# Output products of 512 columns in passes over two tiles of tokens, and mean and deviation spread over the partitions by two products a block

## The chip, the cores and the metric

The program runs on one core of a Trainium2 chip. The metric is the device time of one execution in microseconds (us). The median of three executions of the kernel before is 2492.5 us (2488.48 to 2496.61).

## The reference, cut to what matters

The input x has 4 sequences of 1024 tokens with 1024 numbers each. It is normalised without gains (`xn`), and the output is `x + attention(xn) + experts(xn)`.

- Attention: `q = xn @ Wq`, `v = xn @ Wv`; `s[t] = lam * s[t-1] + v[t]` along a sequence, with one `lam` a head; `y = q * s`. Then y is normalised over its 1024 numbers (mean mu, variance var), `y = (y - mu) * rsqrt(var + 1e-5) * ln_g + ln_b`, multiplied by `silu(xn @ Wg)`, and multiplied by `Wo`.
- Experts: a router picks 8 of 64 experts for a token. Each expert takes at most 128 of its tokens, computes `h = silu(xg @ w1.T) * (xg @ v1.T)` (384 numbers), then `h @ w2`, and adds the weighted result to the output rows of its tokens.

All products are to be of fp32 quality.

## The kernel before, in words

Every operand of a product is split in a high part (fp32r, written by ScalarE) and a low part (raw less high, written by VectorE or GpSimd). A product is three matmuls into one PSUM accumulation: high by high, high by low, low by high (`three`, L1542 to L1546). K is 1024, so 8 slices k of 128 rows.

The 4096 tokens are walked in 8 blocks j of 512 (4 tiles of 128). In a block, in the order in which TensorE's program is written:

1. The v and q stage (`vq_proj`, L1613): 16 products of 128 channels by 512 tokens (24 matmuls each) into the two banks of `psA`. VectorE runs the scan on v and multiplies by q into `yb` (channels on partitions, tokens on columns). ScalarE squares, GpSimd sums.
2. The gate stage (`g_proj`, L1620): 8 products for Wg. `token_sums` turns the sums into mean and mean square a token, `token_var` and `token_six` compute m (mean) and d (deviation, sqrt(var + eps)) a token and place them, high and low, in six columns of `tok6`; `token_turn` transposes them into `tok6T`. Since 1/d is a factor of the whole row, it is left to the end: with `z = ((y - m) * g + d * b) * gate`, the output is `z @ Wo / d`. So `shift` (L1701) makes, for each chunk m of 128 channels, one 512 column product of `ln6T` (the gains and offsets in six rows) by `tok6T`, which is `d * b - m * g`; `shift_in` (L1196) computes `yb * g + that` in one VectorE instruction that reads PSUM, `gate_in` (L1203) multiplies by the gate, `z_hi_of` and `z_lo_of` split z (chunk 7's low part is VectorE's, `lo_z7`).
3. The out stage (`out_proj`, L1628): z is the stationary side (128 channels by 128 tokens), Wo the moving one. For each quarter mm of the output columns (256 of 1024) and each pair w of token tiles: 2 tiles x 8 k x 3 matmuls of 256 columns into one bank of `psA`, half a bank a tile. `out_copy` (L804) moves a bank to `ot` with the factor 1/d, and `add_out` (L618) adds 512 tokens x 256 columns to the output in DRAM by an accumulating DMA of GpSimd's queue.

Beside the attention's stages run 64 experts: 10 to a block from block 2 on (4 in v and q, 2 in the gate stage, 4 in the out stage), 3 in the out stage of block 1. The expert steps stand between the attention's products in a fixed order: `hidden_turn` (transposes of h), `output_mm` (18 matmuls of 512 columns), `gather_turn` (8 transposes), `hidden_mm` (48 matmuls of 384 columns). An expert's weights come in 6 pieces of 768 KB through three slots (`ew_raw`, `ew_hi`, `ew_lo`); the attention's weights come in pieces of 512 KB through two slots (`pw_raw`, `pw_hi`, `pw_lo`). SyncE's queue issues these loads, each after a wait for the slot.

Block 0 also has the routing of all 32 token tiles between its products, and between block 0's out stage and block 1's gate stage VectorE sorts the routing keys: `list8` (a MAX8 and a MATCH_REPLACE8 over 2048 columns, 16 rounds), then `merge8` (16 rounds over 256 columns). TensorE transposes the merged list (L1780), VectorE computes the index table, and only then can the first expert's rows be gathered. In block 0 the out stage has no experts in it; its weights lie in further rooms (`pw2`, `pw3`), which overlay the buffers of x and the experts.

The order on each engine is the written one; engines meet at semaphores. The waits that matter here: a product waits for the low part of its weights (`s_pwlo`) and for its bank (`s_vq` or `s_go`), the out stage also for z (`s_zlo`, `s_zlo7`), `output_mm` for `shift_in` of the whole block in the gate stage (both use `psY`), `masks_turn` (L1581) for VectorE's top 8 of the last tiles.

Of the kernel before, what the change touches and what calls it, by code (L numbers as in the profile page):

```python
# [52 lines left out]
def build(nc, x, proj_w, ew, router, lam_in, g_in, b_in, out, batches, seq, experts):  # L53
# [16 lines left out]
    with ctx:  # L70
# [8 lines left out]
        slab_bytes = 207 * 1024  # L79
# [13 lines left out]
        ones = place("ones", [P, P], F32)  # L93
# [24 lines left out]
        pw_lo = place("pw_lo", [P, 2, KC, P], F32R)  # L118
        st = place("st", [P, TB], F32)
        sq = place("sq", [P, TB], F32)  # L120
        y_sum = place("y_sum", [P, TB], F32)
        q_sum = place("q_sum", [P, TB], F32)
        tok6 = place("tok6", [P, NT, P], F32)
        tok6T = place("tok6T", [P, TB], F32R)
        ln6T = place("ln6T", [P, KC, P], F32R)
        xn = place("xn", [P, KC, P], F32)
        at_o = top[0]
        ot = place("ot", [P, 2 * NT, 2 * P], F32)
# [6 lines left out]
        at_gT = top[0]  # L135
        gT_hi = place("gT_hi", [P, KC, P], F32R)
        gT_lo = place("gT_lo", [P, KC, P], F32R)
        at_sh = top[0]
        assert at_sh == at_gT + 2 * KC * P * 4
# [5 lines left out]
        end_e = top[0]  # L145
        assert end_e - at_sh >= 2 * KC * P * 4
# [3 lines left out]
        pw2_hi = place("pw2_hi", [P, 2, KC, P], F32R, at_x)  # L150
        pw2_lo = place("pw2_lo", [P, 2, KC, P], F32R, at_x + 2 * KC * P * 4)
        pw3_hi = nc.alloc_sbuf_tensor_at("pw3_hi", [P, 2, KC, P], F32R, offset=slab_at + at_gT, align_bytes=4)
        pw3_lo = nc.alloc_sbuf_tensor_at("pw3_lo", [P, 2, KC, P], F32R, offset=slab_at + at_sh, align_bytes=4)
        rt_hi = place("rt_hi", [P, 2, KC, P], F32R)
        rt_lo = place("rt_lo", [P, 2, KC, P], F32R)
# [19 lines left out]
        ln2 = place("ln2", [P, 2, KC], F32)  # L175
        ln2_hi = place("ln2_hi", [P, 2, KC], F32R)
        ln6 = place("ln6", [P, KC, P], F32)
# [68 lines left out]
        s_ln = sem("s_ln")  # L246
        s_lnT = sem("s_lnT")
        s_l6 = sem("s_l6")
        s_sh = sem("s_sh")
        s_t = sem("s_t")  # L250
# [60 lines left out]
        def each_out(eng, last, body):  # L311

            if last:
                with eng.Fori(0, KC // 2 - 2) as mm:
                    body(mm, True, True)
                body(KC // 2 - 2, False, True)
                body(KC // 2 - 1, False, False)
            else:
                with eng.Fori(0, KC // 2) as mm:
                    body(mm, True, True)  # L320
# [13 lines left out]
        def out_room(mm):  # L334

            return ((pw2_hi, pw2_lo), (pw_hi, pw_lo), (pw3_hi, pw3_lo), (pw2_hi, pw2_lo))[mm]
# [6 lines left out]
        ROUNDS_OUT = (0, 2, 2, 2)  # L343
        ROUNDS_VQ = (3, 3, 2, 2)
# [12 lines left out]
        def _(sp):  # L357
# [51 lines left out]
            def load_first(e):  # L409

                for c in range(3):
                    load_piece(e, c, PIECES * e - 2 + c)
# [43 lines left out]
            for mm in range(KC // 2):  # L456
                if mm == 1:
                    store_w(NB - 1)
                next_xn(0, mm)
                for w in range(2):  # L460
                    load_proj(0, 3 * KC + 2 * mm + w + 4)
                for i in range(2):
                    copy_x(copied + 2 * mm + i)
# [12 lines left out]
            for mm in range(KC // 2):  # L476
                if mm == 0:
                    sp.wait_ge(s_ix, 5)
                    sp.wait_ge(s_wst, 16 * NTILE)
                    sp.wait_ge(s_spare, 48)  # L480
                    for c in range(3):
                        load_piece(0, c)
                next_xn(1, mm)
                if mm > 0:
                    load_rest(mm)
                for w in range(2):
                    load_proj(1, 3 * KC + 2 * mm + w + 4)
                if mm == 0:
                    load_rest(0)
                    load_first(1)  # L490
                else:
# [1408 lines left out]
```

## Time and profile before

| | |
|---|---|
| median of three executions | 2492.5 us |
| profiled execution | 2492.86 us |
| its span (first to last instruction) | 2491.2 us |
| mean granted TensorE clock | 0.992 of full speed |
| TensorE matmul busy | 2440.3 us (98%) |
| VectorE busy | 1628.7 us (65%) |
| ScalarE busy | 1317.3 us (53%) |
| GpSimd busy | 673.4 us (27%) |
| DMA, mean | 243 GB/s |

In a row by stretch stand: its ends and length; busy time (and instructions) of TensorE's matmuls, its weight loads, VectorE, ScalarE and GpSimd; TensorE's granted clock; the DMA engines' busy share; GB/s. A row by group has the line, engine, operation, tiles and shapes, count, busy us, mean ns, and the idle time before it with what ended it. A row of the timeline has start, duration and instruction.

The profile is of one execution; 1.7 us of its time lie outside its span. Ends of matmuls are modelled and overlap, so the time that a matmul costs is read from one start to the next, not from its duration.

### The profile page before, as it was taken

Reading aid. Unit: us, or ns where it says so; the run is one execution under the profiler, and the core shown is the slowest. Engines: PE = TensorE matmul, PEld = TensorE weight load, DVE = VectorE, ACT = ScalarE, POOL = GpSimd, SP = SyncE. Lnnn points to the kernel's source line nnn. Section 1 sums busy time; section 2 is a strip of 40 time slices with the busy share of each in tenths; the row PEclk is TensorE's granted clock in tenths of the full one; section 3 lists DMA queues with packets and bytes.
Section 4 is the critical chain, followed back from the end, with each engine's and each line's share of the span. In section 5 each row is a group of like instructions: output and inputs, shape, how many; then the busy total and the mean of one; then the engine's idle time right before and its main releaser. Section 6 shows DMA issues by size and latency. Waiting matters only on the chain.

```text
span 2491.2 us, 39295 instructions
## 1 busy us (share of the span) xinstructions
PE 2440.3 (98%) x13649; PEld 2185.7 (88%) x13649; DVE 1628.7 (65%) x1689; ACT 1317.3 (53%) x1499; POOL 673.4 (27%) x523
## 2 busy tenths in 40 slices
PE   7999999999999999999999999999999999999997
PEld 7888977898889988899888998889988889988897
DVE  7776897666566666666666766656666566656654
ACT  5557323555456644556445665545654556544554
POOL 3221122223222232222223222322223222323311
PEclk9999999999999999999999999999999999999998
DMA  7786854797668976679766698666986669867686
GB/s 275 261 310 201 243 194 162 240 326 225 203 223 264 304 228 232 221 239 310 252 227 213 214 327 266 218 216 213 307 289 193 233 225 287 277 227 233 208 275 167
DMA packets 151790, 605.74 MB, mean 243 GB/s; under 512 B 20592, under 2 KB 37040, under 8 KB 151216
## 3 DMA queue, kind: packets, MB, share of 16 engines
q1 hardware_dynamic: 116304, 518.91, 57.7%
q0 software_dynamic: 35424, 86.00, 16.7%
q8 instruction: 39, 0.64, 0.1%
q14 instruction: 23, 0.19, 0.0%
HBM read 520.89 MB, written 100.70 MB: 250 GB/s over the span
## 4 chain that ended last, share of the span: by engine, by line
PE 84%; DVE 9%; ACT 3%; DMA 3%; issue 1%; SPq 0%; POOL 0%; DVEq 0%; ACTq 0%; POOLq 0%
PE psA L1544 17%; PE psA L1545 17%; PE psA L1546 17%; PE psH L1544 6%; PE psH L1546 6%; PE psH L1545 6%; PE psY L1544 4%; PE psY L1545 4%; PE psY L1546 4%; DVE ew_lo L1157 3%; PE psX L1651 2%; ACT ew_hi L753 2%; PE psY L1576 1%; DVE keys L1147 1%; DVE l L1144 1%; DVE pw_lo L1152 1%
## 5 line engine op out<-in xcount | busy, mean ns | idle before, releaser
L1157 DVE TENSOR_TENSOR ew_lo<-ew_raw,ew_hi 128x1536 fp32r<-128x1536 f32 x384 | 694.6, 1817 | 331.1 <-ACT ew_hi L753 320.5
L753 ACT ACTIVATE ew_hi<-ew_raw 128x1536 fp32r<-128x1536 f32 x384 | 568.3, 1484 | 162.5 <-DMA ew_raw<-ew_dram 134.4
L1544 PE MATMUL psA<-xT_hi,pw_hi 128*128 128x512 f32 (+1 forms) x1544 | 610.2, 395 | 4.9 <-DVE pw_lo L1152 2.7
L747 ACT ACTIVATE pw_hi<-pw_raw 128x1024 fp32r<-128x1024 f32 x254 | 266.2, 1059 | 640.4 <-PE psA L1546 637.5
L1545 PE MATMUL psA<-xT_lo,pw_hi 128*128 128x512 f32 (+1 forms) x1544 | 602.2, 390 | 0.0
L1546 PE MATMUL psA<-xT_hi,pw_lo 128*128 128x512 f32 (+1 forms) x1544 | 602.0, 390 | 0.0
L1152 DVE TENSOR_TENSOR pw_lo<-pw_raw,pw_hi 128x1024 fp32r<-128x1024 f32 x256 | 315.3, 1242 | 146.7 <-ACT pw_hi L747 141.3
L1544 PE MATMUL psH<-ew_hi,gT_hi 128*128 128x384 f32 x1024 | 345.5, 337 | 4.6 <-DVE ew_lo L1157 4.6
L1544 PEld LDWEIGHTS psA<-xT_hi,pw_hi 128*128 128x128 f32 x1544 | 291.4, 189 | 63.1 <-issue 6.7
L1546 PEld LDWEIGHTS psA<-xT_hi,pw_lo 128*128 128x128 f32 x1544 | 291.2, 189 | 61.7
L1546 PE MATMUL psH<-ew_hi,gT_lo 128*128 128x384 f32 x1024 | 343.0, 335 | 0.0
L1545 PE MATMUL psH<-ew_lo,gT_hi 128*128 128x384 f32 x1024 | 342.7, 335 | 0.0
L1545 PEld LDWEIGHTS psA<-xT_lo,pw_hi 128*128 128x128 f32 x1544 | 291.6, 189 | 56.1
L1544 PE MATMUL psA<-pw_hi,z_hi 128*128 128x256 f32 x1024 | 296.1, 289 | 3.6 <-POOL z_lo L615 2.2
L1546 PE MATMUL psA<-pw_hi,z_lo 128*128 128x256 f32 x1024 | 291.2, 284 | 0.0
L1545 PE MATMUL psA<-pw_lo,z_hi 128*128 128x256 f32 x1024 | 291.0, 284 | 0.0
L601 POOL TENSOR_TENSOR y_sum<-y_sum,yb 128x512 f32<-128x512 f32 x64 | 117.2, 1831 | 546.4 <-ACT sq L790 546.4
L594 POOL DMA_INDIRECT out_dram<-ys,s_idx x64 | 118.6, 1854 | 327.7 <-ACT w_tab L777 303.4
L1544 PEld LDWEIGHTS psH<-ew_hi,gT_hi 128*128 128x128 f32 x1024 | 192.3, 188 | 14.2 <-DVE ew_lo L1157 12.6
L1544 PEld LDWEIGHTS psA<-pw_hi,z_hi 128*128 128x128 f32 x1024 | 197.6, 193 | 4.4 <-POOL z_lo L615 2.4
L1545 PEld LDWEIGHTS psA<-pw_lo,z_hi 128*128 128x128 f32 x1024 | 197.8, 193 | 0.1
L1546 PEld LDWEIGHTS psA<-pw_hi,z_lo 128*128 128x128 f32 x1024 | 197.6, 193 | 0.0
(161 smaller groups left out, 3318.9 us busy)
## 6 DMA issues: line engine op xcount, KB each, us to landing
ew_raw<-ew_dram SPq DMA_DIRECT2D x384, 768.0 KB, 6.3
pw_raw<-proj_w_dram SPq DMA_DIRECT2D x256, 512.0 KB, 5.3
xn_scratch<-xt SPq DMA_DIRECT2D x33, 512.0 KB, 4.7
xt<-x_dram SPq DMA_DIRECT2D x32, 512.0 KB, 6.0
out_dram<-x_dram SPq DMA_DIRECT2D x32, 512.0 KB, 6.2
out_dram<-ot POOLq DMA_DIRECT2D x32, 512.0 KB, 12.5
xn<-xn_turned SPq DMA_DIRECT2D x29, 512.0 KB, 4.2
xn_turned<-xraw SPq DMA_DIRECT2D x28, 512.0 KB, 5.1
```

What stands on the lines that cost most here:

```text
L594: pool.indirect_dma_start(out, bass.IndirectOffsetOnAxis(ap=s_idx[:, 0:1], axis=0), ys[:, :], None, compute_op=ALU.add).then_inc(s_sc, 16)
L601: pool.tensor_tensor(y_sum[:, :], y_sum[:, :], yb[:, 2 * mm + h, :], ALU.add)
L747: act.activation(dst[:, slot, :, :], pw_raw[:, slot, :, :], ACT.Copy).then_inc(s_pwhi, 1)
L753: act.activation(ew_hi[:, c % 3, :], ew_raw[:, c % 3, :], ACT.Copy).then_inc(s_ewhi, 1)
L1144: dve.max(into[:, c], src).then_inc(steps, 1)
L1147: dve.match_replace(src, into[:, c], src, -1.0).then_inc(steps, 1)
L1152: dve.tensor_tensor(dst[1][:, slot, :, :], pw_raw[:, slot, :, :], dst[0][:, slot, :, :].bitcast(F32), ALU.subtract).then_inc(s_pwlo, 1)
L1157: dve.tensor_tensor(ew_lo[:, c % 3, :], ew_raw[:, c % 3, :], ew_hi[:, c % 3, :].bitcast(F32), ALU.subtract).then_inc(s_ewlo, 1)
L1544: pe.matmul(dst, l_hi, r_hi_, start=first, stop=False)
L1545: pe.matmul(dst, l_hi, r_lo_, start=False, stop=False)
L1546: return pe.matmul(dst, l_lo, r_hi_, start=False, stop=last)
L1651: o = pe.transpose(psX[:, k // 4, (k % 4) * P:(k % 4 + 1) * P], xg[:, k * P:(k + 1) * P], ident[:, :])
```

## The change

- Output products: a pass takes one half of the output columns (h, 512 columns) and two tiles of tokens (u). Each of its 16 pairs of k and tile is three matmuls of 512 columns, a tile to a bank of `psA`. There are 4 passes a block, and a pass goes through four pieces q of weights, two k each; Wo is cut on the host so that a piece is 2 k x 512 columns. `out_copy` comes once a pass, after the third expert piece, and copies both banks; in block 0 odd passes use `psH`. `add_out` adds 256 tokens x 512 columns.
- Weights: `pw2` becomes a room of its own for the first two pieces of each half, filled in the gate stage (half 0) and in pass 1 (half 1); `pw` holds the other two. The out stage loads 6 pieces in place of 8, in passes 1, 2 and 3, and the gate stage two more.
- Mean and deviation: the 8 products with `ln6T` give way to 2 a block (`spread`): a product with a matrix of ones and zeros (`sel`) puts m on all partitions, another d. ScalarE makes `d * b` of a chunk into `bs`, with two places (`std_of`), VectorE subtracts m from a chunk (`center`), and `shift_in` is then `yb * g + bs`. `gain_rows` and 6 of 8 transposes at the start go.
- Order: in an out pass `hidden` (and `silu_h`) comes before the split of the last expert piece; `std_of` stands in ScalarE's gate stage; block 1's first gather is issued earlier, its index table is computed in the gate stage, and TensorE's transpose of the merged list stands before the last gate product. In block 0's out stage ScalarE takes the next tokens (`take_xT`) before `logits_lo`, VectorE `xT_lo_of` before `take_logits` and `top8_of`. The 16 rounds of `list8` are spread 4 + 12 (before: 6 + 10) over block 0's out stage and block 1's v and q stage.

```diff
-            def out_proj(j, mm, w, tiles=(0, 1), weights=(pw_hi, pw_lo), ks=range(KC)):
 ...
-                        o = three(psA[:, w, t * 2 * P:(t + 1) * 2 * P], z_hi[:, k, c], z_lo[:, k, c],
-                                  weights[0][:, :, k, :], weights[1][:, :, k, :], k == 0, k == KC - 1)
+            def out_pass(j, h, u, pieces):
+                for q in pieces:
+                    if q == 0:
+                        copies = max(2 * h + u - 1, 0) if isinstance(j, int) and j == 0 else 2 * h + u
+                        pe.wait_ge(s_go, 16 * j + 8 + 2 * copies + 2)
+                    if u == 0:
+                        pe.wait_ge(s_zlo, (KC - 1) * j + min(2 * q + 2, KC - 1))
+                        if q == 3:
+                            pe.wait_ge(s_zlo7, j + 1)
+                        pe.wait_ge(s_pwlo, NPJ * j + 3 * KC + 4 * h + q + 1)
 ...
+                    for kk in range(2):
+                        k = 2 * q + kk
+                        cols = slice(kk * TB, (kk + 1) * TB)
+                        for t in range(2):
+                            toks = slice((2 * u + t) * P, (2 * u + t + 1) * P)
+                            o = three(bank_out(j, u)[:, t, :], z_hi[:, k, toks], z_lo[:, k, toks],
+                                      hi[:, cols], lo[:, cols], k == 0, k == KC - 1)
+                    if q % 2 == 1:
+                        o.then_inc(s_pj, 1)
 ...
-            def shift(j, m):
-                if m > 1:
-                    pe.wait_ge(s_t, KC * j + m - 1)
 ...
+            def spread(j):
+                pe.wait_ge(s_t6, j + 1)
+                ps = psH if isinstance(j, int) and j == 0 else psY
+                for i in range(2):
+                    o = pe.matmul(ps[:, i, :], sel[:, i, :], tok6T[:, :], start=True, stop=True)
+                o.then_inc(s_sh, 1)
 ...
+            def run_out(j, e, h, u):
+                out_pass(j, h, u, range(2))
                 hidden_turn(e)
-                out_proj(j, mm, 1, (0,))
+                out_pass(j, h, u, (2,))
                 output_mm(e)
                 gather_turn(e + 1)
-                out_proj(j, mm, 1, (1,))
+                out_pass(j, h, u, (3,))
                 hidden_mm(e + 1)
 ...
+            def center(j, m):
+                ps = psH if isinstance(j, int) and j == 0 else psY
+                dve.tensor_tensor(yb[:, m, :], yb[:, m, :], ps[:, 0, :], ALU.subtract).then_inc(s_u, 1)
 ...
+            def std_of(j, m):
+                if isinstance(m, int) and m == 0:
+                    act.wait_ge(s_sh, j + 1)
+                if m >= 2:
+                    act.wait_ge(s_t, KC * j + m - 1)
+                ps = psH if isinstance(j, int) and j == 0 else psY
+                act.activation(bs[:, m % 2, :], ps[:, 1, :], ACT.Copy, scale=ln_b[:, m:m + 1]).then_inc(s_bs, 1)
 ...
+            def out_copy(j, i):
+                act.wait_ge(s_pj, n2(j, i, 1) + 1)
+                wait_alone(act, s_acc, 16 * (4 * j + i + 1))
+                for t in range(2):
+                    s = i % 2 * 2 + t
+                    act.activation(ot[:, s, :], bank_out(j, i)[:, t, :], ACT.Copy,
+                                   scale=col[:, 4, s:s + 1]).then_inc(s_go, 1)
```

## Rows read from the trace of the kernel before

**Rows 1.** The page: TensorE's busy time, and the chain that ended last by engine.
```profile
PE 2440.3 (98%) x13649; PEld 2185.7 (88%) x13649; DVE 1628.7 (65%) x1689; ACT 1317.3 (53%) x1499; POOL 673.4 (27%) x523
...
PE 84%; DVE 9%; ACT 3%; DMA 3%; issue 1%; SPq 0%; POOL 0%; DVEq 0%; ACTq 0%; POOLq 0%
```

**Rows 2.** Groups by line and form: out products (one line of three) and shift products.
```profile
L1544 PE MATMUL psA<-pw_hi,z_hi 128*128 128x256 f32 x1024 | 296.1, 289 | 3.6 <-POOL z_lo L615 2.2 <-DVE z_lo L1238 1.3
...
L1706 PE MATMUL psY<-tok6T,ln6T 128*128 128x512 f32 x56 | 18.2, 400 | 0.0
```

**Rows 3.** Timeline of TensorE, out stage of block 2: start, duration, instruction.
```profile
820.15 0.28 PE L1544 MATMUL psA<-pw_hi,z_hi 128*128 128x256 f32 x1
...
825.89 0.49 PE L1671 MATMUL psX<-ident,hh 128*128 128x128 f32 x3
826.14 0.36 PE L1544 MATMUL psA<-pw_hi,z_hi 128*128 128x256 f32 x1
...
829.10 0.40 PE L1544 MATMUL psY<-ew_hi,hT_hi 128*128 128x512 f32 x1
```

**Rows 4.** Timeline of TensorE, v/q and gate stage of block 2: products of 512 columns.
```profile
561.88 0.49 PE L1544 MATMUL psA<-xT_hi,pw_hi 128*128 128x512 f32 x1
...
567.46 0.39 PE L1544 MATMUL psY<-ew_hi,hT_hi 128*128 128x512 f32 x1
...
719.03 0.39 PE L1544 MATMUL psA<-xT_hi,pw_hi 128*128 128x512 f32 x1
...
724.47 0.62 PE L1706 MATMUL psY<-tok6T,ln6T 128*128 128x512 f32 x2
724.92 0.33 PE L1544 MATMUL psH<-ew_hi,gT_hi 128*128 128x384 f32 x1
```

**Rows 5.** Busy time by stretch: block 2's gate and out stage, block 1's v/q, 255 to 263.
```profile
694.60:769.70 75.10, 75.10 (x376) 65.44 (x375) 49.19 (x52) 39.44 (x49) 21.08 (x17) 1.00 0.66 214
769.70:870.20 100.50, 100.50 (x693) 97.23 (x692) 65.05 (x48) 64.64 (x76) 23.36 (x18) 1.00 0.92 292
...
306.30:397.10 90.80, 88.10 (x386) 71.77 (x385) 83.18 (x70) 21.05 (x24) 23.48 (x17) 1.00 0.62 216
...
255.00:263.00 8.00, 6.70 (x32) 6.47 (x31) 5.31 (x15) 0.38 (x1) 0.00 (x0) 0.50 0.61 210
```

**Rows 6.** Groups in block 2's gate stage: nearest rows for the added instructions.
```profile
L1200 DVE SCALAR_TENSOR_TENSOR yb<-yb,ln_g,psY 128x512 f32<-128x512 f32 x8 | 5.7, 740 | 0.0
...
L794 ACT ACTIVATE gb<-psA 128x512 f32<-128x512 f32 x8 | 4.6, 581 | 0.0
```

**Rows 7.** Groups of VectorE from 300 to 400 us, in block 1's v/q stage.
```profile
L1144 DVE MAX8 l<-keys 128x8 f32<-128x2048 f32 x12 | 27.4, 2287 | 0.0
L1147 DVE MATCH_REPLACE8 keys<-l,keys 128x2048 f32<-128x2048 f32 x11 | 25.0, 2276 | 0.0
...
L1193 DVE TENSOR_TENSOR yb<-psA,st 128x512 f32<-128x512 f32 x8 | 5.5, 691 | 3.0 <-PE psA L1546 2.8
```

**Rows 8.** Timeline, block 0's out stage: top 8's last step, next tokens, masks' transposes.
```profile
263.64 0.29 DVE L1096 TENSOR_SCALAR mk<-rep 128x256 f32<-128x256 f32 x1
...
263.70 1.06 ACT L875 ACTIVATE xT_hi<-xn 128x1024 fp32r<-128x1024 f32 x1 [2.43 <-DMA xn<-xn_turned]
...
271.30 0.60 PE L1584 MATMUL psY<-ident,mk 128*128 128x128 f32 x4
```

**Rows 9.** Timeline, block 1: the last merge, and the first expert's transposes.
```profile
439.03 0.41 DVE L1144 MAX8 lf<-l 64x8 f32<-64x256 f32 x1
...
462.21 0.41 PE L1651 MATMUL psX<-ident,xg 128*128 128x128 f32 x2 [3.07 <-DMA xg<-xn_scratch,g_idx]
```

**Rows 10.** Timeline of TensorE, the last expert.
```profile
2472.09 0.90 PE L1671 MATMUL psX<-ident,hh 128*128 128x128 f32 x3 [3.96 <-DVE hh L1162]
2474.16 0.79 PE L1544 MATMUL psY<-ew_hi,hT_hi 128*128 128x512 f32 x1 [1.17 <-DVE hT_lo L1172]
```

**Rows 11.** Waits, whole span: ScalarE for the experts' weights.
```profile
ACT ew_hi L753 <- DMA ew_raw<-ew_dram: 134.4, 60, 4.5
```

More of the change, by code:

```diff
@@ L118, in build @@
         pw_lo = place("pw_lo", [P, 2, KC, P], F32R)
+        pw2_hi = place("pw2_hi", [P, 2, KC, P], F32R)
+        pw2_lo = place("pw2_lo", [P, 2, KC, P], F32R)
+        rt_hi, rt_lo = pw2_hi, pw2_lo
+        at_st = top[0]
         st = place("st", [P, TB], F32)
+        tok6T = place("tok6T", [P, TB], F32R, at_st)
         sq = place("sq", [P, TB], F32)
+        at_ysum = top[0]
         y_sum = place("y_sum", [P, TB], F32)
@@ L309, in each_vq, with each_out @@
                 body(mm)
[L311 to L320, printed above, removed]
+        def each_out(last, body):
+            for i in range(KC // 2):
+                body(i, not last or i < KC // 2 - 1)
         def tiles_under(p):
@@ L689, in run, with outp @@
                     z_lo_of(j, m)
-                def outp(mm, loads, splits):
+                def outp(mm, more):
                     scatter(e0 + 6 + mm, 4 * j + mm)
-                    if splits:
+                    if more:
                         gather_next(e0 + 7 + mm)
@@ L1456, in run_out @@
                 piece_lo(e + 1, 2)
-                if splits:
-                    proj_lo(n2(j, mm, 2), 0)
-                    proj_lo(n2(j, mm, 3), 1)
-                hidden_part(e + 1)
-            run_out(1, 1, 2, True, False)
-            run_out(1, 2, 3, True, False)
+                if i == 3 and not last:
+                    for w in range(2):
+                        proj_lo(n2(j, 4, w), w)
+                piece_lo(e + 1, 3)
+                piece_lo(e + 1, 4)
+                hidden(e + 1)
+                piece_lo(e + 1, 5)
+            for i in range(1, 4):
+                run_out(1, i - 1, i, False)
             def run(j, e0, last):
@@ L1532, in run @@
                 hidden(e + 2)
-                each_out(dve, last, lambda mm, loads, splits: run_out(j, e0 + 6 + mm, mm, splits, last))
+                each_out(last, lambda i, more: run_out(j, e0 + 6 + i, i, last))
             phases(dve, run)
@@ L1856, in run @@
                 hidden_mm(e + 2)
-                each_out(pe, last, lambda mm, loads, splits: run_out(j, e0 + 6 + mm, mm, last))
+                with pe.Fori(0, 2) as h:
+                    for u in range(2):
+                        run_out(j, e0 + 6 + 2 * h + u, h, u)
             phases(pe, run)
```

472 lines of the change are left out of this document (223 added, 249 removed).

## The prediction, as it went on record

> **What bounds the kernel now.** The busy shares come first: TensorE is busy for 2440.3 of 2491.2 us, VectorE for 65%, ScalarE for 53%; the chain of waits is TensorE for 84% [rows 1]. Then the stretches: in block 2's gate and out stage, which stand for those of blocks 2 to 7, TensorE never rests, at a clock of 1.00, while VectorE is busy 49 of 75 us and 65 of 100 us [rows 5]. So there time is what TensorE's instructions cost from start to start, and other engines count only where they come late. The exceptions are the routing in blocks 0 and 1, where VectorE is nearly full (83 of 91 us in block 1's v and q stage, [rows 5]), and the last expert [rows 10]. The timeline then gives the costs from start to start: 48 out matmuls of 256 columns take 825.89 - 820.15 = 5.74 us, 119.6 ns each [rows 3]; 24 matmuls of 512 columns take 724.47 - 719.03 = 5.44 us, 226.7 ns each [rows 4]. Two of 256 cost 239.2 ns, so one of 512 saves 12.5 ns over them.
>
> **Part 1, the output products.** 3072 matmuls of 256 columns (three lines of 1024, [rows 2]) become 1536 of 512. A pass: 96 x 0.1196 = 11.48 us becomes 48 x 0.2267 = 10.88 us, 0.60 less. Behind transposes the first matmul comes later: 24 of 512 columns then take 5.58 us, 0.14 over 5.44 [rows 4], and 24 of 256 take 2.96 us, 0.09 over 2.87 [rows 3]. There are two such places in a pass before and after, so 2 x 0.05 = 0.10 goes back: 0.50 us a pass, 2.0 us a block. The new matmuls have the shape of the v and q products (128 x 128 stationary, 512 columns moving), so I take those products' price. Bounds: 0 (nothing saved) to 0.60 a pass.
>
> The rows above show 119.6 and 226.7 ns. The Trainium skill (TensorE: Matmul & The Clock Gate, Back-to-back issue gap) gives columns / 2.4 + 2.5 ns for an isolated stream: 109.2 ns for 256 and 215.8 for 512. By that, a pair would save 2.6 ns and part 1 about 4 us in all 1536 pairs, not 19. It speaks against this part; the trace disagrees by 10.4 and 10.9 ns, a cost a matmul that does not grow with the columns, and half of which goes when matmuls are joined. Its rival is below.
>
> **Part 2, mean and deviation.** A block has 8 products of 512 columns in the gate stage (56 in blocks 1 to 7, [rows 2]); a pair costs 0.45 us [rows 4]. Two remain: three pairs less are 1.35 us a block.  Added: 8 centres on VectorE, nearest row 0.69 us (a sum of yb and PSUM, [rows 7]), at most 0.74 [rows 6]: 5.5 us; 8 copies with a factor on ScalarE, nearest row 0.58 [rows 6]: 4.6 us. Two more splits of weights move into the gate stage as well: VectorE then has 49.2 + 5.5 + about 2.5 = 57 of 73.7 us, ScalarE 39.4 + 4.6 + 2 = 46. That is room. What hides them is TensorE's own time, but they are in chains: centre and shift of chunks 4 to 7 stand before the split of the next gate weights and before the low part of h, which `output_mm` waits for; and `output_mm` waits for all of `shift_in`. After `hidden` VectorE has 4 centres and 4 shifts (5.7 us), a split of weights and h's low part (about 1.8) to do, 7.5 us; ScalarE's `bs` for chunks 6 and 7 goes step by step with it, perhaps 1 us more. TensorE meanwhile has two gate products and transposes, 2 x 5.44 + 0.25 = 11.1 us. It fits with 2 to 3 us over. If it did not, each us late would cost one a block. I take 0.2 us a block for small lateness; bounds 0 and 3.
>
> **Part 3, where the passes meet the other engines.** A pass now needs both banks of psA at its start, so both copies of the pass before must be done. They stand behind the split of expert piece 3, which needs the first quarter of `hidden_mm`. `hidden_mm` is 48 matmuls of 384 columns, about 8.3 us between passes; a quarter is 2.1, the split 1.5, two copies 1.2 to 1.4: about 5 of 8.3 us, with 3 over. The copies are the same work as before. Pass 2 needs pieces whose slot came free only at the end of pass 1: 2 high parts and 2 low parts lie between `hidden` and its third piece, which TensorE wants 5.4 us into the pass. With the last expert piece ahead of them this is tight; I take 0.2 us a block, bounds 0 and 1.5. DMA: the out stage is 92% busy at 292 GB/s [rows 5], and ScalarE waits 134.4 us in all for expert pieces [rows 11], so far without cost to TensorE. A block's out stage now carries two loads of 512 KB less (some 1 of 29 MB), and the accumulating write has half as many rows, twice as long. It is 2% shorter. I take nothing for it; bounds: a gain of none (TensorE does not wait for it now) and a loss of 1 us a pass.
>
> Blocks 2 to 7: 6 x (2.0 + 1.35 - 0.4) = 17.7 us.
>
> **Blocks 0 and 1.** TensorE's savings alone are 8 x 0.50 + 2 x 1.35 = 6.7 us, and some 0.6 us of six transposes. Against it stand three changes of order.
> - Block 0's masks: the top 8 was done at 263.93 and TensorE came at 271.30 [rows 8]. Now TensorE comes after one pass of 10.9 us and some 2 us of router products, near 261.3, and VectorE's top 8 stands behind the low part of the next tokens, whose high part waited for a DMA until 263.70 [rows 8]: 263.7 + 1.1 (high) + 1.2 (low) + 2.6 (logits and top 8) = 268.5. TensorE waits for some 7 us. Three passes then take 32.6 us where 288 matmuls took 34.6, so the stage ends near 301.6 instead of 306.3, if the clock holds. It was at 0.50 (1.2 of 2.4 GHz) from 255 to 263 after waits [rows 5], so I put 2.5 us on it: 2 us gained.
> - Sorting: a round of `list8` is 2.29 + 2.28 = 4.57 us [rows 7]. Twelve rounds fall into block 1's v and q stage in place of ten. A quarter with three rounds has 13.7 us of them and 8.7 us of scan, products and splits, 22.4 in all, against 4 x 5.44 = 21.8 for TensorE. Two more such quarters cost 1 us or so.
> - Merges: VectorE's last merge began at 439.03 [rows 9], about when TensorE was through with its seventh gate product, and TensorE now wants it before the eighth. With the centres and two slots of weights ahead of it, TensorE waits for 3 to 4 us there, but the first gather is issued before block 1's out stage, where TensorE stood still until 462.21 [rows 9], so most of that wait is taken from this one.
> I take 4 us for both blocks together; bounds -3 and +7.
>
> **The end.** The last expert's transposes wait for hh for 3.96 us, behind the split of its sixth piece, and the next products another 1.17 us [rows 10]. Now silu and hh come first. Up to 2.5 us of the first wait go, but h's low part is then late behind the sixth piece. I take 2 us; bounds 0 and 5 (with the clock up).
>
> **The sum.** 17.7 + 4 + 2 = 23.7 us, some 24. Off the profiled execution's 2492.86 us that is 2469 us. That execution is 0.4 us over the median, so nothing is changed for it: 2469.
>
> **The rivals.**
> - Early blocks and new waits give much of it back: pass 2 late by 1.5 us and the gate stage by 1.5 in each of six blocks, nothing gained in blocks 0 and 1. For it: two tight places, and each wait is behind ScalarE and VectorE in turn. Against: the margins above. 2492.9 - 6 x 0.75 - 2 = 2486; half of it gives 2478.
> - Joining columns saves hardly anything: only the columns count. As a mechanism here: the 119.6 ns would be no fixed cost but one of the weights' loads or of a half bank. Then part 1 gives 0 and the rest 24 - 6 x 2.0 - 2 = 10: 2483. Against it: both prices are read in runs without waits. The rule of the skill quoted above would come to this.
> - Slower: the two banks. A pass can't start until both copies are done, and they wait behind expert piece 3. If piece 3 lands more than 3 us late, TensorE stands still in each of 24 passes. Rows 5 and 11 speak for it: DMA at 92%, waits of up to 4.5 us for a piece. Against it: these waits are for later pieces, and the stage has less to load. The point from which it decides is 1 us of standing still a pass; at 2 us it is 24 x 2 = 48 us against a gain of 24, 2517.
> - The gain of the early blocks whole and the clock up at the end: 21 + 7 + 5 = 33, 2460.
>
> **How the numbers follow.** The forecast (2461 to 2476) has 0.62; the early blocks' rival and mixtures up to 2485 0.17, beyond it 0.04; columns that save nothing 0.06; the two banks 0.06 (slower by more than 0.3% 0.05); the whole gain 0.05. What a measurement can tell from no change is about 0.3%, 7.5 us: faster is under 2485. Range 2459 to 2482; faster 0.89, same 0.06, slower 0.05.
>
> **What would show it.** In the trace after: out matmuls of 512 columns at 226 to 228 ns from start to start, a step of an out stage (pass and expert) 0.5 us shorter than before, 16 spreading products in all; a gate stage about 1.3 us shorter; TensorE waiting for the masks near 261 us for some 7 us; the wait at the last expert smaller. It would be wrong if a wait for `s_go` or for a low part stands at the head of passes in blocks 2 to 7, or if 512 columns cost 239 ns.

## The result, and the profile after

The changed kernel takes 2512.9 us (median of 5 executions, 2509.1 to 2520.4), the kernel before in the same comparison 2492.5 us (2488.5 to 2499.9): a ratio of 1.0079, 95% interval 1.0052 to 1.0106. It is slower by 20 us, where 24 us less were forecast; the time lies outside the range of 2459 to 2482. The profiled execution has a span of 2507.8 us (2491.2 before) and a time of 2509.82 us.

The page of the changed kernel, its busy times, instruction queues and chain (they answer to [rows 1]):
```profile
PE 2422.1 (97%) x12059; PEld 2095.8 (84%) x12059; DVE 1667.8 (67%) x1747; ACT 1341.8 (54%) x1499; POOL 710.2 (28%) x527
...
q8 instruction: 70, 1.15, 0.2%
q14 instruction: 25, 0.20, 0.0%
...
PE 78%; DVE 10%; ACT 5%; DMA 4%; issue 3%; SPq 0%; POOL 0%; ACTq 0%; DVEq 0%; POOLq 0%
```
TensorE is busy for 18.2 us less, while the span is 16.6 us longer: TensorE does less and stands still for more. "issue" (time in which an engine waits for nothing that the profile shows) has grown from 1% of the chain to 3%, and queue q8, which brings instructions, carries 70 packets of 16384 bytes, where the kernel before has:
```profile
q8 instruction: 39, 0.64, 0.1%
q14 instruction: 23, 0.19, 0.0%
```

The waits of TensorE in the changed kernel: what it waited for, us in total, times, the longest.
```profile
PE psA L1585 <- issue: 18.4, 5, 4.5
PE psX L1600 <- ACT xt L735: 17.5, 4, 10.5
PE psA L1585 <- DVE pw_lo L1196: 8.4, 12, 1.7
...
PE psY L1625 <- DVE mk L1140: 5.2, 1, 5.2
...
PE psX L1816 <- DVE lf L1188: 2.6, 1, 2.6
```
The first line is new: 18.4 us in five waits that are no wait for another engine or a transfer. Four of them, 17.4 us together, are the same place, TensorE's jump from the end of its loop over blocks back to the head. The timeline there, behind block 3 (start, duration, instruction):
```profile
1193.27 0.34 PE L1587 MATMUL psH<-ew_hi,gT_lo 128*128 128x384 f32 x1
1198.10 0.79 PE L1585 MATMUL psA<-xT_hi,pw_hi 128*128 128x512 f32 x1 [4.49 <-issue]
1198.69 0.63 PE L1586 MATMUL psA<-xT_lo,pw_hi 128*128 128x512 f32 x1
```
and the stretches around it (us, then busy time and instructions of PE, PEld, DVE, ACT, POOL, the granted clock, DMA share, GB/s):
```profile
1193.80:1198.10 4.30, 0.00 (x0) 0.01 (x1) 2.46 (x3) 1.82 (x2) 1.63 (x3) 0.99 1.03 412
1198.10:1201.50 3.40, 3.40 (x8) 2.73 (x9) 0.00 (x0) 0.00 (x0) 0.00 (x0) 0.51 1.07 322
1201.50:1206.00 4.50, 4.50 (x21) 3.70 (x21) 0.46 (x1) 0.58 (x1) 0.00 (x0) 1.00 0.80 264
```
The idle costs twice: TensorE stands still for 4.3 us, and behind the idle the clock is at its lower level (0.51, 1.2 of 2.4 GHz) for 3.4 us, in which eight matmuls of 512 columns are done instead of fifteen.

The jump has a record of its own, as an instruction of TensorE's queue. Below it stands for the changed kernel, the kernel before and e2 (of the next section): executions, then ns of the shortest, the median and the longest. The shortest is the last time round, where the loop ends and nothing is jumped.
```profile
L298 PEldq COMPARE_BRANCH  x5: 67/5957/6117, 866.5 to 2164.2; - x5
...
L303 PEldq COMPARE_BRANCH  x5: 67/209/209, 868.1 to 2146.2; - x5
...
L303 PEldq COMPARE_BRANCH  x5: 67/6177/6415, 871.6 to 2176.7; - x5
```
The jump takes 0.21 us before and some 6 us in the changed kernel, of which TensorE hides the first part behind matmuls already queued. Behind block 3 it starts at 1191.16, the one instruction packet of the idle starts at 1194.95 and takes 0.95 us, and the next instruction of the queue comes at 1197.33.

The trace has a comparison of its own. Blocks 2 to 5 end in the jump back; block 6 runs on into block 7's code without one. From the first product of the out stage to the next block's first projection it is 104.1, 104.1, 104.3 and 104.5 us in blocks 2 to 5 and 100.0 us in block 6 (100.5 in the kernel before); the projections that follow take 151.1 to 151.4 us behind a jump and 149.7 us without.

Against that, both savings of the forecast are there. The out matmuls of 512 columns, two groups of the view by form, and the spreading matmuls (16 where 64 were: the 56 of [rows 2] and 8 in block 0):
```profile
L1585 PE MATMUL psA<-pw_hi,z_hi 128*128 128x512 f32 x480 | 192.6, 401 | 7.4 <-DVE pw_lo L1196 6.8 <-ACT gb L816 0.7
...
L1585 PE MATMUL psH<-pw_hi,z_hi 128*128 128x512 f32 x32 | 13.1, 408 | 0.0
...
L1753 PE MATMUL psY<-tok6T,sel 128*128 128x512 f32 x14 | 4.3, 389 | 0.0
...
L1753 PE MATMUL psH<-tok6T,sel 128*128 128x512 f32 x2 | 0.7, 424 | 0.0
```
The start of a pass, and the transposes and the next piece behind its first 24 matmuls, to set beside [rows 3]:
```profile
793.87 0.39 PE L1585 MATMUL psA<-pw_hi,z_hi 128*128 128x512 f32 x1
...
799.36 0.49 PE L1718 MATMUL psX<-ident,hh 128*128 128x128 f32 x3
799.60 0.49 PE L1585 MATMUL psA<-pw_hi,z_hi 128*128 128x512 f32 x1
```
24 matmuls take 799.36 - 793.87 = 5.49 us, 228.7 ns each. Block 2's gate and out stage (they answer to the first two of [rows 5]):
```profile
694.20:768.50 74.30, 74.18 (x371) 64.44 (x370) 56.41 (x62) 45.77 (x59) 25.94 (x17) 1.00 0.66 216
769.30:868.60 99.30, 98.63 (x501) 86.88 (x499) 63.74 (x47) 61.94 (x66) 25.30 (x19) 1.00 0.94 298
```

To see where time goes, the span is cut at TensorE's own instructions. All numbers in us, from the starts in the timelines (the end of TensorE is modelled, and good to 0.1 or 0.2 us); e1 to e10 are the runs of the next section.

| kernel | to the first token sums | blocks 0 and 1 from there | blocks 2 to 7 | end of TensorE to end of span | span |
|---|---|---|---|---|---|
| before | 185.1 | 365.6 | 1930.6 | 9.9 | 2491.2 |
| changed | 186.3 | 365.0 | 1943.2 | 13.4 | 2507.8 |
| e1, blocks written out | 192.7 | 370.8 | 1915.7 | 13.2 | 2492.4 |
| e2, old kernel, longer body | 188.6 | 365.1 | 1957.7 | 9.5 | 2520.9 |
| e5, old kernel, blocks written out | 189.5 | 363.2 | 1929.5 | 9.9 | 2492.1 |
| e4, order of block 0 | 181.6 | 365.8 | 1949.7 | 13.7 | 2510.8 |
| e6, pass 2's weights earlier | 182.8 | 368.2 | 1910.7 | 13.8 | 2475.5 |
| e7, order and rounds | 180.0 | 365.4 | 1921.2 | 13.2 | 2479.9 |
| e8, GpSimd in a loop | 187.1 | 365.6 | 1914.8 | 13.6 | 2481.1 |
| e10, old kernel, helpers written out | 184.2 | 363.2 | 1930.0 | 10.2 | 2487.6 |
| e9, all mended | 187.6 | 361.1 | 1909.5 | 13.6 | 2471.8 |

The first column is the same work in every kernel but for six transposes that the changed one leaves out; that it varies by 12.7 us from profile to profile is a measure of how much of a single profile's early part means nothing. The other columns vary too where the code is the same: blocks 0 and 1 take 365.0, 370.8, 368.2 and 365.6 us in the changed kernel, e1, e6 and e8, and blocks 2 to 7 take 1914.8, 1915.7 and 1921.2 in e8, e1 and e7, and 1943.2 and 1949.7 in the changed kernel and e4. A difference of under some 6.5 us between two single profiles is thus not shown by them alone.

### The profile page after: what moved, and what is told of

It reads as the page before. It is cut to its first block, busy times and chain, and to the rows that moved or that the text cites. A ratio compares the mean times of both kernels' runs of the same rounds, so it can differ in the third digit from the quotient of the medians.

```text
span 2507.8 us, 35514 instructions
## 1 busy us (share of the span) xinstructions
PE 2422.1 (97%) x12059; PEld 2095.8 (84%) x12059; DVE 1667.8 (67%) x1747; ACT 1341.8 (54%) x1499; POOL 710.2 (28%) x527
## 4 chain that ended last, share of the span: by engine, by line
PE 78%; DVE 10%; ACT 5%; DMA 4%; issue 3%; SPq 0%; POOL 0%; ACTq 0%; DVEq 0%; POOLq 0%
PE psA L1585 16%; PE psA L1586 16%; PE psA L1587 16%; PE psH L1585 5%; PE psH L1587 5%; PE psH L1586 5%; DVE ew_lo L1201 4%; PE psY L1585 3%; PE psY L1587 3%; PE psY L1586 3%; ACT ew_hi L775 3%; DMA ew_raw<-ew_dram 2%; PE psX L1698 2%; PE psY L1617 1%; DVE pw_lo L1196 1%
## 5 line engine op out<-in xcount | busy, mean ns | idle before, releaser
L1585 PE MATMUL psA<-xT_hi,pw_hi 128*128 128x512 f32 (+1 forms) x1544 | 615.0, 398 | 23.7 <-issue 18.4
L1196 DVE TENSOR_TENSOR pw_lo<-pw_raw,pw_hi 128x1024 fp32r<-128x1024 f32 x256 | 324.4, 1277 | 102.5 <-ACT pw_hi L769 97.1
L1585 PE MATMUL psA<-pw_hi,z_hi 128*128 128x512 f32 x480 | 192.6, 401 | 7.4 <-DVE pw_lo L1196 6.8
L1586 PEld LDWEIGHTS psH<-ew_lo,gT_hi 128*128 128x128 f32 x1024 | 192.3, 188 | 1.7
L1587 PEld LDWEIGHTS psH<-ew_hi,gT_lo 128*128 128x128 f32 x1024 | 192.2, 188 | 0.0
L1586 PE MATMUL psA<-pw_lo,z_hi 128*128 128x512 f32 x480 | 188.0, 392 | 0.0
L1587 PE MATMUL psA<-pw_hi,z_lo 128*128 128x512 f32 x480 | 187.7, 391 | 0.0
L1230 DVE TENSOR_TENSOR_SCAN st<-lam,start,psA 128x512 f32<-128x512 f32 x64 | 81.9, 1280 | 153.3 <-PE psA L1587 152.9
```

The source lines that it names most:

```text
L1196: dve.tensor_tensor(dst[1][:, slot, :, :], pw_raw[:, slot, :, :], dst[0][:, slot, :, :].bitcast(F32), ALU.subtract).then_inc(s_pwlo, 1)
L1230: dve.tensor_tensor_scan(st[:, :], lam[:, bass.ds(m, 1)].to_broadcast([P, TB]), psA[:, 0, :], start[:, bass.ds(m, 1)], ALU.mult, ALU.add). ...
L1585: pe.matmul(dst, l_hi, r_hi_, start=first, stop=False)
L1586: pe.matmul(dst, l_hi, r_lo_, start=False, stop=False)
L1587: return pe.matmul(dst, l_lo, r_hi_, start=False, stop=last)
```

## The experiments

**e1: TensorE's blocks written out.** In the changed kernel, TensorE alone:
```
-            phases(pe, run)
+            for j in range(2, NB):
+                run(j, first_expert(j), j == NB - 1)
```


> The changed kernel with TensorE's loop over blocks 2 to 6 written out; nothing else differs. Fetch theory (the changed loop body, some 783 products of code against 720 before, is fetched again behind each jump back): the four idles of 4.1 to 4.5 us labelled issue, at 868.60, 1193.27, 1517.63 and 1842.43, and the half-clock projections behind them (12.6 against 10.9 us) go, 4 x 6.2 = 25 us less: profiled span about 2483, median about 2488. Rival (the idle stands for a wait the profile does not name, a DMA or an engine at the block boundary): the idles stay and the time is 2510 to 2516. A third way: straight code has to be fetched as well, the idle is spread over the blocks and part of the 25 us stays.

Measured: 2483.8 us (10 executions), a ratio to before of 0.9965, interval 0.9954 to 0.9976. That is 29 us less than the changed kernel, from an edit that changes no matmul, no wait and no order: the jumps go, and with them steps of TensorE's queue that compute with the block's number. The four idles are gone; where the jump was, in the same stretch of time, the clock stays up:
```profile
1189.90:1198.10 8.20, 8.20 (x48) 7.98 (x47) 7.30 (x6) 6.79 (x7) 3.67 (x3) 1.00 0.94 234
1198.10:1206.00 7.90, 7.90 (x38) 6.69 (x38) 4.33 (x5) 3.04 (x3) 2.31 (x3) 1.00 1.04 391
```
Straight code has to be fetched too (60 instruction packets). Of TensorE's waits with "issue" one is left, 0.9 us, where there were five with 18.4.

**e2: the old kernel with a longer loop body.** TensorE alone; the executed matmuls and waits and their order are those of the kernel before.
```
-                each_out(pe, last, lambda mm, loads, splits: run_out(j, e0 + 6 + mm, mm, last))
+                with pe.Fori(0, 2) as h:
+                    for u in range(2):
+                        run_out(j, e0 + 6 + 2 * h + u, 2 * h + u, last)
```


> The kernel before, TensorE's out stage written as a loop of two over two expert steps in place of a loop of four over one; every instruction executed is the same, in the same order. TensorE's loop body over blocks grows from some 720 to some 893 products of code. Fetch theory: an idle of 4 us or more labelled issue at the four jumps back, and half clock behind each: +4 x 6.2 = 25 us, about 2517, and instruction packets in every block. Rival (the idle comes from the new order of the out stage, not from the size of the code): no change, 2490 to 2496.

Measured: 2520.8 us, ratio 1.0111 (1.0094 to 1.0127), 29 us slower than before. Its waits and the place behind block 3:
```profile
PE psA L1544 <- issue: 18.3, 4, 4.8
```
```profile
1204.40 0.79 PE L1544 MATMUL psA<-xT_hi,pw_hi 128*128 128x512 f32 x1 [4.28 <-issue]
```
So neither the wide matmuls nor the order of passes is needed for the idle: TensorE's longer loop body is enough, at nearly the same price with 893 matmuls of code as with 791. (Counted in the code, a block has 173 matmuls in a quarter of v and q, which is a loop of its own, 368 in the changed gate stage and 250 in the changed out stage; before they were 173, 374 and 173, in all 720. The 783 of e1's expectation counts 360 in the gate stage, but 8 `shift` matmuls went and 2 came.) In the kernel before, no packet of q8 moves from 779.7 to 2154.9 us; the changed kernel has nine in each turn of the loop and e2 ten. Between the kernel before and e2 only TensorE's code differs, so these are packets of TensorE's code.

One thing is not separated: both kernels with the idle have the out stage as a loop of two over two steps, both without it as a loop of four over one. No run has the longer body with the old inner loop.

**e5: the control.** The edit of e1 in the kernel before.

> Control: the kernel before with TensorE's loop over blocks 2 to 6 written out. Fetch theory: its loop body is not fetched again (no instruction packets after 800 us), so nothing is to be gained: 2488 to 2495. If every jump back costs, whatever the size of the body, it falls below 2485; if straight code is slower to fetch than a loop that stays in place, it rises above 2500.

Measured: 2493.0 us, ratio 1.0004 (0.9995 to 1.0014). The old body of 720 matmuls jumps back for nothing, and straight code costs nothing either, though it raises the instruction packets from 39 to 62. A packet count alone is therefore no sign of loss; the idle behind "issue" is.

**e4: the order of block 0.** ScalarE and VectorE in block 0 only: the last logits and top 8 ahead of the next tokens' split, and `z_hi` a turn later in the gate stage.
```
-                take_xT(0, mm)
                 if mm == 0:
                     logits_lo(NB - 1)
+                take_xT(0, mm)
+                if mm == 0:
                     exp_of(NB - 1)
...
+                if m == 3:
                     z_hi_of(0, 0)
-                if m >= 2:
-                    z_hi_of(0, m - 1)
+                if m >= 3:
+                    z_hi_of(0, m - 2)
+            z_hi_of(0, KC - 2)
```


> The changed kernel with two orders of block 0 undone or mended, in the loop over blocks nothing. (a) In the first out turn ScalarE copies the last logits before it waits for the xn tile, and VectorE does the last top-8 before xT_lo, as in the kernel before: the masks' turn no longer waits for mk (5.22 us at 267.78). (b) In the gate stage z_hi follows the gate one turn later, so that ScalarE does not stand 4.70 us at 217 before the next normalise: the 2.76 us wait of the transposes and the half clock behind it go. Theory (these two waits are the path): out stage of block 0 starts at about 250 in place of 255.2, and takes 48 to 50 us in place of 53.9; block 1 starts 8 to 10 us earlier, median about 2503. Rival: something else ends last there (the projection weights or the xn load) and less than 4 us is left of it.

Measured: 2511.6 us, ratio 1.0073 (1.0057 to 1.0089): no more than 1.3 us less than the changed kernel, inside the uncertainty. Both waits went, as expected: gate stage 66.3 us in place of 68.9, out stage 50.5 in place of 53.9, 6.0 us gained. Block 1 gave all of it back: its v and q stage took 99.0 us in place of 95.3, its gate and out stage 3.2 more. VectorE there, in e4:
```profile
310.00:330.00 20.00, 18.07 (x78) 14.00 (x76) 19.79 (x18) 4.60 (x6) 2.93 (x3) 1.00 0.45 157
330.00:350.00 20.00, 19.49 (x86) 16.18 (x87) 19.83 (x17) 4.70 (x5) 6.68 (x4) 1.00 0.66 233
350.00:370.00 20.00, 19.67 (x88) 15.96 (x87) 19.83 (x18) 4.88 (x6) 6.77 (x4) 1.00 0.55 191
370.00:390.00 20.00, 19.68 (x87) 16.00 (x86) 19.79 (x19) 5.08 (x6) 6.77 (x4) 1.00 0.65 234
```
VectorE (the third pair) works 79.2 of 80 us. TensorE came earlier to a stage in which VectorE is full: it waits for VectorE for 5.6 us there, where it waits 1.5 in the changed kernel. That VectorE bounds the stage is shown in part only, for TensorE too is busy for 76.9 of these 80 us, and its clock is at 0.85 on average in the first 11.6 us of the stage, where it is at 1.00 in the changed kernel.

**e6: pass 2's weights earlier.** On top of e1, on ScalarE (and with `proj_lo` on VectorE alike):
```
-                if i == 2:
-                    for w in range(2):
-                        proj_hi(None, w, half2(j, 3), n2(j, 1, 1) + 1)
                 hT_hi_of(e)
...
                 out_copy(j, i)
+                if i == 1:
+                    for w in range(2):
+                        proj_hi(None, w, half2(j, 3), n2(j, 1, 1) + 1)
                 piece_hi(e + 1, 4)
```


> TensorE's blocks written out (as in the run before, 2483.8 us), and the conversion of the third and fourth weight pair of the second half moved from the head of expert step 2 to step 1 of the out stage, right behind the copy of pass 1 out of PSUM, on ScalarE and VectorE. Theory: the wait of 0.7 to 1.3 us for pw_lo in pass 2 of every block goes (it stands behind an expert piece whose DMA lands at 820.8 and on which these conversions do not depend), 6 blocks x 0.9 = 5.4 us: about 2478.5. Rival: the pieces of the expert become as late as the conversions were (silu, hh, then the turn), and the wait moves to the turn of hh: 2483 to 2485.

Measured: 2480.7 us, ratio 0.9960 (0.9947 to 0.9974), 3 us less than e1 by the medians, but the intervals of the two ratios overlap, so the time alone doesn't show it. The trace does: in pass 2 of blocks 2 to 7 the changed kernel waits for `pw_lo` six times, 4.6 us in all, e1 4.2 and e7 7.0, and e6 and e9 not once; blocks 2 to 7 take 1910.7 us in place of 1915.7. What it removes is seen in the changed kernel's timelines of ScalarE, VectorE and TensorE in pass 2 of block 2, here of all three:
```profile
820.79 1.49 ACT L775 ACTIVATE ew_hi<-ew_raw 128x1536 fp32r<-128x1536 f32 x1 [1.49 <-DMA ew_raw<-ew_dram]
822.19 1.99 ACT L769 ACTIVATE pw_hi<-pw_raw 128x1024 fp32r<-128x1024 f32 x2
...
822.31 1.76 DVE L1201 TENSOR_TENSOR ew_lo<-ew_raw,ew_hi 128x1536 fp32r<-128x1536 f32 x1 [1.70 <-ACT ew_hi L775]
823.99 1.22 DVE L1196 TENSOR_TENSOR pw_lo<-pw_raw,pw_hi 128x1024 fp32r<-128x1024 f32 x1
...
825.26 0.50 PE L1585 MATMUL psA<-pw_hi,z_hi 128*128 128x512 f32 x1 [0.67 <-DVE pw_lo L1196]
```
Read upward from TensorE: it waits for a low part, which stands behind an expert piece on VectorE, which ScalarE could only convert when its DMA had landed, at 820.79. Weights that had long been there were queued behind a late transfer. In e6 the same product starts right behind the transposes:
```profile
824.21 0.49 PE L1718 MATMUL psX<-ident,hh 128*128 128x128 f32 x3
824.45 0.49 PE L1585 MATMUL psA<-pw_hi,z_hi 128*128 128x512 f32 x1
```

**e7: order of block 0, and a round of the lists moved.** On top of e1 and e4:
```
-        ROUNDS_OUT = (0, 1, 1, 2)
-        ROUNDS_VQ = (3, 3, 3, 3)
+        ROUNDS_OUT = (0, 2, 1, 2)
+        ROUNDS_VQ = (3, 3, 3, 2)
```


> TensorE's blocks written out, the order of block 0 mended as in the run e4, and one of the 12 rounds of top-8 and replace (4.65 us each) that VectorE does in the projection stage of block 1 moved into an idle of VectorE in the out stage of block 0 (270 to 278 in e4). Theory: VectorE (19.8 us busy in every 20 from 310 to 390) bounds block 1's projections, and this is what took back the 6 us that e4 gained in block 0; one round less there gives 4.7 us, so blocks 0 and 1 take 4 to 6 us less than in the changed kernel (364.97 from the first sums to block 2): about 2478. Rival: the lists bound nothing, the projections' 95 to 99 us come from PE's own half clock, and the time stays at 2482 to 2485.

Measured: 2478.1 us, ratio 0.9944 (0.9929 to 0.9959), 5.7 us less than e1, as the theory has it, by medians whose ratios' intervals just overlap. The stages don't bear it out: blocks 0 and 1 take 365.4 us, 5.3 less than in e1's profile, but the profiles of the changed kernel and of e8, without the edit, have 365.0 and 365.6, and block 1's v and q stage is still 98.7 us. What a round less did was to end VectorE's full stretch near 387, where in e4 it lasted beyond 390; TensorE had been held up at the stage's beginning, from 297 to 340. How much of blocks 0 and 1 is bound by VectorE, and how much is the clock's history, is not settled by single profiles.

**e8: GpSimd's out stage in a loop.** On top of e1, one execution, for the end alone.

> TensorE's blocks written out, and GpSimd's four out turns of a block put back into a loop, as they were in the kernel before. Looked at for the end alone: from the last scatter's issue to the end of the span it is 8.2 us in the kernel before (8.2 and 7.8 in its two variants) and 11.5 to 12.0 in all three runs with the changed code. Theory: it is GpSimd's written-out code that makes the end late, then it is 8.2 again. Rival: another engine or the scatter itself, then 11.5.

Measured: 2482.8 us, and 11.9 us from the last scatter (issued at 2469.15) to the end of the span at 2481.1. The theory fell.

**e10: the old kernel with the helpers' out stage written out.**

> The kernel before with the four out turns of a block written out on SyncE, GpSimd, ScalarE and VectorE, as the changed kernel has them; TensorE keeps its loop. It is looked at for the end, from the last scatter's issue to the end of the span: 8.2 us in the kernel before, 11.5 to 12.0 in every run with the changed code, 11.9 with GpSimd alone rolled up. Theory (the written-out code of ScalarE, VectorE or SyncE makes the end late): 11.5 to 12, and the time rises by some 3.5 us to 2494 to 2496. Rival (the new transfer or another part of the change does it): 8.2 and 2491.

Measured: 2491.8 us, ratio 1.0000 (0.9989 to 1.0010); from the last scatter (2479.06) to the end of the span (2487.6) 8.5 us. It fell too: the size of the other four engines' code costs nothing here, at the end or in the loop.

**e9: all mended.** On top of e1, e4, e6 and e7, in short:
```
-        MERGE_G = (3, 3, 3, 3, 3, 1, 0, 0)
+        MERGE_G = (3, 4, 4, 4, 1, 0, 0, 0)
...
+                    if mm == 3 and a == 5:
+                        sp.wait_ge(s_ext, LISTED)
+                        sp.dma_start(l2[:, SLOTS:2 * SLOTS], l1[SEL:2 * SEL, :]).then_inc(s_l2, 16)
                     load_proj(1, 4 * mm + a + 2)
...
+                if i == 3 and last:
+                    hT_lo_of(e + 1)
                 piece_lo(e + 1, 5)
```


> The changed kernel with everything found so far: TensorE's blocks written out, the order of block 0 mended, one round of the lists moved into the out stage of block 0 and another ahead of its last xT_lo, pass 2's weights converted earlier; and in block 1 the lists' transfer sent one projection earlier with the merges spread 3, 4, 4, 4, 1 over the gates (the lf transpose then waits no 2.5 us and no half clock of 2.6 us stands behind it), the weights of pass 0's second half and gT ahead of what they stood behind (1.6 and 2.3 us); in the last expert hT ahead of the last piece (2.5 us). Theory: the waits are the path and none is given back: against the run of the blocks written out (2483.8) 3 for pass 2, 5.7 for blocks 0 and 1 as in e7, 5 for lf, 3 for the two waits, 2.5 at the end, 2464 to 2468. Rival: VectorE bounds blocks 0 and 1 in total, so that only pass 2 and the end count on top of e7: 2472 to 2476.

Measured: 2464.7 us, ratio 0.9891 (0.9874 to 0.9909): 27.7 us faster than the kernel before and 48 us faster than the changed one, with the same products. Blocks 0 and 1 take 361.1 us, the least of all. The wait for lf is gone from TensorE's list, but two others near it have grown, from 2.4 and 0.7 us in e7 to:
```profile
PE psA L1598 <- DVE xT_lo L1309: 3.7, 1, 3.7
PE psA L1598 <- ACT gb L817: 2.9, 1, 2.9
```
and the last expert's h waits 1.17 us in place of 2.49.

## Why the prediction was wrong, step by step

The changed profile's span is 16.6 us over that of before where 23.7 less were forecast, a miss of 40.3 us. By the table: 27.5 us with the jumps, 5.0 in pass 2, 3.3 in blocks 0 and 1, 3.5 behind TensorE's end, and 1.2 in the part before the first sums, less 0.2 that blocks 2 to 7 saved beyond the forecast once both are taken away. Each term is a difference of single profiles; the first alone is far above their spread.

- **The step that was not there.** The prediction asked of each added instruction what it costs when it is executed, and never what it costs to have it in the program. TensorE's out stage was one expert step in a loop of four and became two steps in a loop of two; with the spreading products fewer and the passes shorter, the body of the loop over blocks grew from 720 to 791 matmuls. Each of four jumps back then cost 4.1 to 4.5 us of idle (17.4 in all) and 1.4 to 1.7 of lower clock (6.4 in all). With 2.7 us in the gate stages of blocks 3, 5 and 7, which wait 1.0 us each for a low part of an expert's weights that no run with the blocks written out waits for, and 1 us besides, that is 27.5 us by e1's profile (1943.2 - 1915.7), 29 by the medians. e2 makes the loss in the old kernel, e1 takes it out of the new one, and e5 shows that nothing else was gained by taking the loop away. This is shown. That the idle is the fetch of instructions is the reading that fits: the jump's own record grows from 0.21 to 6 us, and only there; a packet of instructions comes while TensorE stands; and the code is brought anew in each turn, eight packets between 1025 and 1225 us, where the kernel before has none. That it is the number of instructions in the body that decides, and not the form of the inner loop, is argued from this and not shown by a run of its own. The sign of the forecast hung on this step alone: e1, with all the rest, is faster than before. The size did not: e1's 2483.8 us is still above the range of 2459 to 2482.

The instruction queue of the changed kernel in that stretch, from 1025 to 1225 us:
```profile
q8 instruction: 8, 0.13, 0.2%
```
The Trainium skill (Runtime: NRT & Kernel Launch, Instruction fetch mechanics) says that a taken branch to code outside the two pages (512 instructions) that an engine holds forces a DMA fetch before execution goes on. The idle at the changed kernel's jump agrees; the old kernel's jump, over 720 matmuls and as many weight loads, would have had to stand still too, and its record is 0.21 us and e5 measured no loss there. The same section of the Trainium skill also gives TensorE room for 2048 instructions. If a loop body below that size stayed there, both would: the trace has 1440 and 1582 matmuls and weight loads and some 80 to 90 other steps of the queue in a body, and the second was brought anew in every turn.

- **Part 1, the columns: right.** 0.50 us a pass was forecast, 2.0 a block. In e6, where no wait hides it, the out stages of blocks 2 to 6 take 98.5 to 99.2 us against 100.5 to 100.7, 1.4 to 2.0 less. 24 matmuls take 5.49 us where 5.44 had been read off the projections. The rival that only columns count is out.
- **Part 2, the spread: right, a little large.** 1.35 less 0.2 was forecast for a block; the gate stage fell from 69.3 us (first sums to first out matmul) to 68.3 or 68.4 where no wait disturbs it (all six blocks of e1 and e6), 1.0. The load on the others came out as worked out: VectorE 56.4 and ScalarE 45.8 of 74.3 us, where 57 and 46 of 73.7 had been forecast.
- **Part 3, pass 2: mechanism right, size wrong.** 0.2 us a block was taken, with 1.5 as the bound; the wait was 0.3 to 1.1 us at TensorE, 4.6 us in six blocks, and 5.0 by e6, where 1.2 had been taken. The step counted what lies between `hidden` and pass 2's third piece and left out when it could begin: the expert piece ahead of it arrives by DMA only at 820.8. With that taken away, blocks 2 to 7 lost 1930.6 - 1910.7 = 19.9 us, end included. 17.7 + 2 = 19.7 had been forecast with 1.2 for this wait, so 20.9 without it: the savings came 1 us short of it, and that the total fits to 0.2 is two errors that cancel.
- **The two banks: did not happen.** No pass in blocks 2 to 7 waits for the copies. ScalarE's waits for expert pieces fell from 134.4 us [rows 11] to:
```profile
ACT ew_hi L775 <- DMA ew_raw<-ew_dram: 84.9, 64, 3.9
```
  The rival had the right sign with the wrong mechanism, and its 0.06 is not to be counted as foresight.
- **Blocks 0 and 1: 4 us forecast, 0.7 measured,** in profiles that differ by up to 5.8 us there with the same code. The masks' wait was forecast at some 7 us and was 5.22. Missed was the gate stage of block 0, where ScalarE stood 4.70 us for VectorE's `gate_in`, which comes behind the new centres, ahead of the next `xt`, and TensorE then 2.76 us and at the lower clock behind it:
```profile
217.08 1.24 ACT L833 ACTIVATE z_hi<-yb 128x512 fp32r<-128x512 f32 x2 [4.70 <-DVE yb L1260]
```
```profile
224.80 0.76 PE L1600 MATMUL psX<-ident,xt 128*128 128x128 f32 x4 [2.76 <-ACT xt L735]
...
273.39 0.90 PE L1625 MATMUL psY<-ident,mk 128*128 128x128 f32 x3 [5.22 <-DVE mk L1140]
```
  In block 1 the forecast trade took place (the lf transpose waits 2.6 us, the first gather none).
- **The end.** 2 us were forecast. The wait for hh fell from 3.96 [rows 10] to 1.17 us, h's low part then waited 2.49, so about 1.5 came. Behind TensorE's end the span ran 3.5 us longer. From the last scatter's issue to the end of the span it is 11.5 to 12.1 us in all seven profiles with the changed code, and 7.8 to 8.5 in all four with the old. In the changed kernel nothing is busy and no DMA moves for the last 5.3 us:
```profile
2502.50:2507.80 5.30, 0.00 (x0) 0.00 (x0) 0.00 (x0) 0.00 (x0) 0.00 (x0) 0.50 0.00 0
```
  The records show what fills it: a DRAIN at the end of GpSimd's queue, after every other engine is through. In the changed kernel and in the kernel before it is (count, then ns):
```profile
L70 POOLq DRAIN  x1: 4972/4972/4972, 2502.6 to 2502.6; - x1
...
L70 POOLq DRAIN  x1: 1216/1216/1216, 2489.7 to 2489.7; - x1
```
  It takes 4972 ns in all seven profiles with the changed code and 1216 in all four with the old, 3.8 us more. Why it takes longer is open. It is not TensorE's code (e1, e2), nor GpSimd's loop (e8), nor that the helpers' code is longer (e10). The accumulating write with half as many rows, twice as long, remains; that was not tried.
- **Two sums of the rivals.** The first rival's 6 x 0.75 does not follow from its words: 2.0 + 1.35 less 1.5 and 1.5 leaves 0.35 a block, 2.1 us in six, so 2489 and not 2486. The 21 of the last rival has no working; without the two 0.2 it would be 6 x 3.35 = 20.1. Neither decides anything here: the measured time lies beyond all but the two banks' rival, and that one's waits did not come.

## What to carry to other kernels

Count the code of a loop body, engine by engine, before and after an edit that writes out a part of it: here a body of 720 matmuls jumped back for nothing, and one that is a tenth longer cost more at every turn than the edit saved, the clock behind it included. In a profile, look for "issue" idles at the loop's head, read the record of the branch itself and the instruction packets inside the loop, and set a turn with the jump beside one without. A conversion whose data is there must not queue behind one that waits for a late transfer; and time gained ahead of a stage in which another engine is nearly full can be lost there again.

## What the runs showed of the hardware

- TensorE's jump back to a loop's head takes 0.21 us and costs nothing with a body of 720 matmuls (720 weight loads beside them); with 791 or 893 it takes 5.8 to 6.4 us, and TensorE stands for 4.1 to 4.8. The price hardly depends on how far the body is over. It was not tried where between 720 and 791 the edge lies, or whether it is a count of instructions.
- The loop over the smaller body brings no instruction packet in its four jumps back; over the larger bodies it brings nine and ten a turn, 16384 bytes each.
- Straight code of blocks 2 to 7 costs no measurable time on TensorE (ratio 1.0004) with 62 instruction packets in place of 39.
- Behind an idle of 4.3 us, in which the granted clock still shows 0.99, TensorE's clock is at 0.51 for the next 3.4 us. The price of an idle is thus not only its length: 4.3 us cost about 6.
- The DRAIN at the end of GpSimd's queue takes 1.22 us in one form of this kernel and 4.97 us in the other, the same in every profile of a form, with nothing else going on.
